# Global attention on one Trainium2 core: products with the values issued for two key tiles together, at every odd key tile, two and three tiles late

## What is computed

```python
# x: 4 x 1024 x 256, normalised; 16 heads of 16
q = _rope(q); k = _rope(k)
scores = jnp.einsum('blhd,bmhd->bhlm', q, k) * scale
attn = jax.nn.softmax(scores, axis=-1)
out = jnp.einsum('bhlm,bmhd->blhd', attn, v).reshape(B, L, D)
```

## Time and profile before

| | |
|---|---|
| median of 3 runs (lowest to highest) | 2490.89 us (2490.42 to 2492.18) |
| profiled execution, its own time | 2489.49 us |
| its span, first to last instruction | 2487.7 us |
| mean granted TensorE clock | 0.975 of full speed |
| busy: PE / DVE / ACT / POOL | 2340.7 / 1625.5 / 1420.7 / 616.3 us |
| the global attention's exponentials (line 718) | 512, from 187.5 to about 884 us of the span |
| products with the values (line 591) | 2048 records, 191.0 to 884.1 us |
| maxima reductions (line 655) | 1024, 154.1 to 855.5 us |

### The profile page before, as it was taken

The page is one execution under the profiler, slowest core; times in us unless marked ns, Lnnn a source line. Parts: engine busy times, 40 slices in busy tenths (PEclk is TensorE's granted clock), DMA queues, the critical chain, the costliest instruction groups (busy, mean ns, idle before and its releaser), DMA issues. The chain is left out here.

```text
span 2487.7 us, 40290 instructions
## 1 busy us (share of the span) xinstructions
PE 2340.7 (94%) x12576; PEld 1412.1 (57%) x12576; DVE 1625.5 (65%) x3713; ACT 1420.7 (57%) x2634; POOL 616.3 (25%) x484
## 2 busy tenths in 40 slices
PE   7969999999999979899999999999899999999968
PEld 4533333333333357667667667667667667667534
DVE  5778999999999746646646556546645646646326
ACT  2207777777777756547557556457456547557321
POOL 4412100000000044333323323323234233323000
PEclk9969999999999989999999999999999999999989
DMA  4583212111221010000000000000000000000006
GB/s 151 186 245 111 61 52 60 50 46 57 60 60 52 14 41 1 1 1 1 0 0 0 0 0 25 1 9 22 13 1 1 0 0 0 0 0 0 0 21 196
DMA packets 71891, 95.83 MB, mean 39 GB/s; under 512 B 13884, under 2 KB 49168, under 8 KB 71696
## 3 DMA queue, kind: packets, MB, share of 16 engines
q1 hardware_dynamic: 71808, 94.78, 12.5%
HBM read 60.67 MB, written 39.49 MB: 40 GB/s over the span
## 5 line engine op out<-in xcount | busy, mean ns | idle before, releaser
L655 DVE TENSOR_REDUCE maxima<-ps_m 128x1 f32<-128x512 f32 x1024 | 635.1, 684 | 64.0 <-PE ps_m L546 60.0
L718 ACT ACTIVATE probs<-ps_st 128x1024 f32<-128x1024 f32 x512 | 496.1, 1021 | 173.3 <-PE ps_st L578 171.8
L546 PE MATMUL ps_m<-k_st,q_st 48*128 48x512 f32 x1024 | 391.0, 468 | 31.8 <-DMA k_st<-ks 15.8
L578 PE MATMUL ps_st<-q_st,k_st 50*128 50x512 f32 x1024 | 306.7, 426 | 2.9 <-DMA q_st<-max_rows 1.8
L1236 ACT ACTIVATE l_probs<-l_probs,l_neg_max 128x256 f32<-128x256 f32 x512 | 253.5, 496 | 71.6 <-DVE l_neg_max L1365 69.2
L578 PEld LDWEIGHTS ps_st<-q_st,k_st 50*128 50x128 f32 x1024 | 160.6, 186 | 223.9 <-ACT probs L718 190.5
L591 PE MATMUL ps_o<-probs,v_st 128*32 128x512 f32 x2048 | 274.5, 608 | 0.6 <-ACT probs L718 0.6
L1215 ACT COPY p_turned<-ring 128x512 f32<-128x512 f32 x256 | 144.3, 592 | 227.4 <-PE ring L1030 227.4
L546 PEld LDWEIGHTS ps_m<-k_st,q_st 48*128 48x128 f32 x1024 | 172.0, 190 | 148.2 <-DVE maxima L655 125.8
L1365 DVE CUSTOM_DVE_ANT_1 l_probs<-ring,l_mask 128x256 f32<-128x256 f32 x384 | 145.4, 422 | 130.2 <-PE ring L1067 124.2
L990 POOL TENSOR_SCALAR clipped<-sumsq 128x16 f32<-128x16 f32 x64 | 16.2, 253 | 807.1 <-DVE sumsq L1342 807.1
(11 more groups left out here) (152 smaller groups left out, 3980.9 us busy)
## 6 DMA issues: line engine op xcount, KB each, us to landing
qs<-split SPq DMA_DIRECT2D x16, 512.0 KB, 3.5
ks<-split SPq DMA_DIRECT2D x16, 512.0 KB, 5.1
q_st<-qs SPq DMA_DIRECT2D x64, 128.0 KB, 2.6
k_st<-ks SPq DMA_DIRECT2D x64, 128.0 KB, 3.2
o<-o_sb SPq DMA_DIRECT2D x32, 256.0 KB, 2.4
x_in<-in_L_attn_x_dram SPq DMA_DIRECT2D x8, 512.0 KB, 6.3
v<-v_sb SPq DMA_DIRECT2D x16, 256.0 KB, 4.7
q_st<-qs SPq DMA_DIRECT2D x64, 64.0 KB, 2.9
```

What stands on the lines that cost most here:

```text
L546: nc.tensor.matmul(bank(base, use)[:, :], q_st[u][r, qt * P:(qt + 1) * P], k_st[u][r, h * CH:(h + 1) * CH], start=True, stop=True).then_in ...
L578: mm = nc.tensor.matmul(ps_st[j][:, h * CH:(h + 1) * CH], k_st[u][r, kt * P:(kt + 1) * P], q_st[u][r, h * CH:(h + 1) * CH], start=True, st ...
L655: nc.vector.tensor_reduce(maxima[:, par, side(e), tile + e // 4, e % 2:e % 2 + 1], bank(base, k + e)[:, :], AX_X, ALU.max).then_inc(m_used, 1)
L718: nc.scalar.activation(probs[:, kt % 4, j, :], ps_st[j][:, :], ACT.Exp, scale=float(G_DIM) ** -0.5).then_inc(exp_done, 1)
```

## The change

`product` gets the iteration, and waits for the values itself in the first unit of an iteration. A new function, `late_products`, issues at odd kt the products of key tiles kt - 3 and kt - 2 (at kt = 1 those of key tiles 6 and 7 of the unit before) and at even kt nothing. It is called between the two pairs of head 0 and the two pairs of head 1, where before one product stood after all four pairs. The copy of the finished output on ACT moves from kt = 0 to kt = 1, and after the very last key tile two products are issued instead of one.

```diff
+        LAG = 2
...
-                def product(n, kt, u):
-
+                def product(n, kt, i, u):
+
+                    if u == 0:
+                        pe.wait_ge(v_placed, TILES * i + kt + 1)
                     pe.wait_ge(exp_done, 2 * TILES * n + 2 * kt + 2)
...
+                def late_products(i, n, kt, u, first):
+
+                    for lag in (LAG + 1, LAG) if kt % 2 else ():
+                        if kt >= lag:
+                            product(n, kt - lag, i, u)
+                        elif u:
+                            product(n - 1, TILES + kt - lag, i, u - 1)
+                        elif not first:
+                            product(n - 1, TILES + kt - lag, i - 1, NB - 1)
...
-                            for j in range(2):
+                            if kt == TURN:
+                                for e in (0, 1):
+                                    if m:
+                                        maxima_scores(base, *m[e])
+                                late_products(i, n, kt, u, first)
                                 for h in range(2):
-                                    e = 2 * j + h
-                                    if kt == TURN and j == 0:
-                                        if m and h == 0:
-                                            maxima_scores(base, *m[0])
-                                            maxima_scores(base, *m[1])
-                                        scores(n, kt, u, j, h, more1)
-                                    else:
-                                        scores(n, kt, u, j, h, more1)
-                                        if m:
-                                            maxima_scores(base, *m[e])
-                            if u == (1 if kt == 0 else 0):
-
-                                pe.wait_ge(v_placed, TILES * i + (kt - 1) % TILES + 1)
-                            if kt:
-                                product(n, kt - 1, u)
-                            elif u:
-                                product(n - 1, TILES - 1, u - 1)
-                            elif not first:
-                                product(n - 1, TILES - 1, NB - 1)
+                                    scores(n, kt, u, 0, h, more1)
+                            else:
+                                for h in range(2):
+                                    scores(n, kt, u, 0, h, more1)
+                                    if m:
+                                        maxima_scores(base, *m[h])
+                                late_products(i, n, kt, u, first)
+                            for h in range(2):
+                                scores(n, kt, u, 1, h, more1)
+                                if m:
+                                    maxima_scores(base, *m[2 + h])
                         if last and u == NB - 1:
-                            product(n, TILES - 1, u)
+                            for kt in range(TILES - LAG, TILES):
+                                product(n, kt, i, u)
...
-                            if kt == 0:
+                            if kt == LAG - 1:
                                 if u:
                                     copy_o(n - 1, i, u - 1)
```

## The result

The changed kernel is slower: 2696.96 us median of four runs (2671.74 to 2722.12), against 2490.65 for the kernel before. Its executions fall on two levels, 2671.8 twice and 2722.0 twice (mean clock 0.934 and 0.907); the ratio goes by the first level: **1.0729, interval 1.0703 to 1.0754**. The forecast was 2580 (2548 to 2604), slower. The direction and the longer loop were right, but the time lay outside the range: of some 180 us lost the forecast had 89, and what it left out is TensorE's clock.

The account below looks back on a forecast made before the run. The prediction took the bound to be a loop in which PE and DVE wait for each other through three banks. Terms 72 + 12 + 3 + 4 - 2 = 89 us on 2489.49 gave 2578, stated as 2580, range 2548 to 2604.

Parts of the forecast that it names:

- what bounds the kernel: Attention's steady stretch: PE and DVE wait for each other through three banks; a key tile takes 2.70 us.
- the loop's terms: Key tile before the change: 0.75 + 0.42 + 0.99 + 0.54 = 2.70 us, from one train of reductions to the next.
- the second product (0.90): In a batch, the second product adds two groups of 0.45 us, 0.90; bounds 0.85 and 0.99.
- the regular pair (6.00): Two key tiles from batch end to batch end: 6.00 us against 5.41, 0.59 more.
- The turn's pair: Pair where the maxima are turned: 0.6 us longer than a regular one through ACT's chain; 12 us in all.
- kt = 0: Where the bank count starts again, M3 waits for M1's reduction: 0.09 us in 31 units, 3 us.
- A whole unit: Unit of the attention: 4 x 6.00 + 0.6 + 0.09 = 24.7 us, against 21.87 before.
- 122 x 0.59 = 72 us: Loss over the loop's 122 pairs of key tiles, 0.59 us each, the largest term of the sum.
- the end, priced at 4 us: End of the attention, without maxima products: pairs of 5.3 us against 4.41, 0.9 more in five pairs.
- PE is the bound: Rival: busy shares are the truth, each pair saves 0.33 us, 40 us in all, 2451; chance 4%.
- The lead of 0.24: PE's idle before a product's weights, which the rival with 2451 us saves once a pair.
- Slower by much more: Rival: ACT sets the end of each regular pair too, 0.2 to 0.3 us more, over 2605; chance 9%.

Follow-up runs that it names:

- Short reductions: Kernel before, with DVE reducing only the first 256 of each 512 columns of a maxima product: 2427.47 us (0.9766).
- the last kernel: Kernel before with products halved except those issued at kt = 0 and 5 and all of the first unit: 2501.95 us (1.0051).
- Two kernels here: Kernel before with every product halved, output copy at kt = 1: 2543.39 us; with halves except at kt = 0, 5 and the first unit: 2501.95 us.
- the one that gained: Kernel before with products halved, except those issued at kt = 0 and 5, output copy staying at kt = 0: 2476.69 us (0.9947).

## Why the prediction was right and wrong

**Right: what bounds the kernel.** The loop of four reductions, three banks and PE's absence was the bound, and PE was not, for all its 94%. Short reductions took the tile from 2.70 to the 2.44 us that the loop's terms give.

**Right: the second product (0.90) and the regular pair (6.00).** A batch at full clock is 1.854 us, so the second product costs 0.86, between the two bounds; the pair is 5.96. The turn's pair was given 6.6 and took 6.55. Only kt = 0 was priced too low, 0.09 against the 0.33 of the kernel with each such product issued twice. A whole unit was given 24.7 us and takes 24.74 there.

**Failed: that nothing else would change, the clock above all.** The sum took every duration at the full clock of the earlier trace rows and had no term for it, nor did the rivals or the range. The step was "122 x 0.59 = 72 us", with an even tile in which PE has no product. A unit was forecast at 24.7 us and is 27.31 ((1025.3 - 234.0) / 29 = 27.29 by the transposes, which answer to the earlier trace rows):

```profile
L567 PE MATMUL ps_st<-g_ident,max_hl x30: 283/283/283, 234.0 to 1025.3; 128*32 128x128 f32 x30
```

The 2.6 us between are two batches a unit at half clock, 3.07 and 2.84 instead of 1.85, together 2.2, and the maxima product and lead before each, 0.3 longer, together 0.6; that is 2.8, a little more than the difference. Over these 29 units 2.6 each are 75 us.

**Failed by the same step: the end, priced at 4 us.** From the last transpose to the start of the last exponential the changed kernel takes 38.1 us, the kernel before 22.4:

```profile
1025.30:1063.40 38.10, 30.42 (x126) 8.68 (x129) 0.00 (x0) 20.15 (x23) 0.00 (x0) 0.69 0.02 8
```

```profile
860.20:882.60 22.40, 21.52 (x125) 7.19 (x121) 0.00 (x0) 19.10 (x23) 0.00 (x0) 1.00 0.04 14
```

That is 15.7 us in place of 4, with a mean clock of 0.69. The sum had pairs of 5.3 us there. The last one ahead of the fall of the clock, from the batch at 1015.85 to that at 1021.13, does take 5.28, and the ones behind it 6.95 to 8.5. So the step that failed is again the clock. So of the 91 us that the forecast lacked, 75 are in the 29 units, 12 in the end, and 4 in the first two units.

**Rivals.** "PE is the bound" fell with the short reductions. The lead of 0.24 into a product is real, and half of the products no longer have it. It fits the drain that the Trainium skill ("TensorEngine Tiling (Array Packing)", Key Properties) names. Leaving it out saved nothing that the time shows: it lay in time in which PE waits for DVE anyway. "Slower by much more" had the right side and the wrong mechanism: ACT's chain doesn't set the regular pair at full clock.

**What a page says of it.** The Trainium skill, "TensorE: Matmul & The Clock Gate", Loop structure matters more than you think, says that whether matmuls stay warm is set by the loop nest. This case agrees (1.00 before, 0.87 after). Its example is a PE that waits with nothing to do, and the stops of 4 us in the last kernel are such a case. In the changed kernel PE was issuing small matmuls, and its row was busy for 3.34 of the 3.49 us before the clock fell.

## What to carry to other kernels

Where two engines hand a small ring of buffers to each other, write down the loop, and ask of each reordering how long it keeps one of them away: batching two late products saved a switch that cost nothing and doubled the absence that did cost. And when work on TensorE is bunched, look at what is left between the bunches: a stretch with little in it can halve the clock for the dense part behind it. Put a term for the clock in the range of every change that thins out a stretch.

Where a variant misses, look first at where in the loop the time went. Two kernels here lost it only where the loop turns, which their regular tiles could not show, and the count of instruction packets on the page told them from the one that gained.

## What the runs showed of the hardware

- PE's mean clock was below full while its row showed 92 to 99% busy (0.87 at 756.18 of 821 us, 0.57 at 706.82 of 711). With the same score and maxima matmuls, it was 1.00 with a whole product in every tile and 0.57 with a quarter of one in seven tiles of eight.
- Extra matmuls whose results are thrown away made a kernel faster, 2603.65 us with 976 of them against 2671.8 without.
- In two of the kernels instructions were brought in again in every iteration of the loop (96 and 94 packets in q8 instead of 45 to 50), and PE stood still for 2.5 to 4.2 us at five turns of the loop. The clock fell during each stop or within 2 us of its end, for 3 to 51 us.
- A product cut in halves of 256 columns costs 0.57 us each, from its start to the next score matmul, against 0.996 for a whole one: 0.14 us more for the two, and the second lead, 0.3 to 0.4 us from the last maxima matmul to the half product, comes on top.
